# Old keys' probabilities of all four row tiles turned by way of memory, the new keys first in every chunk

## The chip, the core and the metric

One core of one Trainium2 chip. The metric is the device time of one execution in microseconds (us), the median of several runs. TensorE multiplies matrices, VectorE (DVE), ScalarE (ACT) and GpSimd (POOL) work element by element, SyncE (SP) issues every DMA of this kernel, in program order. TensorE writes its results to PSUM banks of 128 x 512 floats; everything else lies in on-chip memory (SBUF) or in DRAM.

## The reference

Four sequences ("batches") of 512 rows of 512 features. Layer norm, attention over 512 context rows (the "old" keys and values) and the 512 rows' own keys and values (the "new" ones), a gated residual, a second layer norm, a feed-forward block with sign weights, and a second residual:

```python
q, k_new, v_new = x @ wq.T, x @ wk.T, x @ wv.T          # x: layer norm of the rows
k = concatenate([k_cache, k_new]); v = concatenate([v_cache, v_new])
attn = softmax(q @ k.T / sqrt(512))
x = x + tanh(g_xattn) * ((attn @ v) @ wo.T)
hidden = relu((layernorm(x) @ sign(up).T) * up_scale)
x = x + tanh(g_ffn) * ((hidden @ sign(down).T) * down_scale * output_scale)
```

## The kernel before

Precision comes from splitting: an operand is kept as a high part, made by ACT (`..., HI`), and a low part, made by DVE or POOL (`..., LO` = value minus high part), and each product is three matmuls (`PASSES`, high-high, high-low, low-high). So each thing that TensorE uses passes through ACT and then DVE.

The program is written out by hand for each engine, batch after batch (`batch(b)`, b = 0 to 3), with semaphores between the engines. In one batch TensorE computes, in this order:

- scores (seven products in the manner of Strassen), whose sums DVE puts into `probs`; ACT makes the exponentials tile by tile in the order 2, 3, 0, 1;
- `v_jobs`: new values 0 and 1, 16 transposes of 128x128 that turn the new keys' probabilities of the four row tiles, values 2 and 3, then 8 transposes for the old keys' probabilities of tiles 0 and 1 (`turn_probs`, `TURN_ORDER`, `turn_job` at L665);
- the attention (L855 on): four chunks e of 128 features, each 12 matmuls over new and 12 over old keys, in two banks `proj[:, e % 2]`, so that chunk 2 can only begin when chunk 0 has been copied out;
- the output projection, 16 pieces of 3 matmuls, the first four of which need chunk 0, the next four chunk 1, and so on (`out_piece`);
- the keys and queries of the next batch, which need that batch's normed rows, `xT`.

Of the old keys' probabilities, tiles 2 and 3 are turned without TensorE. DVE transposes squares of 32x32 (`square_probs`, L1386) into `probs_squares`; SP stores them into DRAM so that the squares change places (`place_squares`, L446: four stores a tile, L451), and loads them again (L457) into `squares_placed`; ACT and DVE split them into `probsT` (`placed_out` L1094, `placed_low` L1390). TensorE waits for that ahead of the first product over old keys.

The layer norm of the next batch uses rows that are loaded already turned. Their means and inverse deviations ("facts") are stored to DRAM by SP (L478), loaded again over all partitions once that store has landed (L483, `all_facts`), and applied by two operations of DVE (`norm_turned`, L1435 and L1438); then ACT splits the result into `xT` (L1181) and DVE makes its low part (`next_rows_low`, L1443). In batch 0 SP comes to the facts after placing the squares (L495, L496), in batches 1 and 2 before. In batch 0 DVE's `norm_turned` stands after its copy of chunk 1 and `next_rows_low` after chunk 2, in batches 1 and 2 after chunks 0 and 1. In batches 1 and 2 DVE also norms and turns four row tiles of an earlier batch (`turn_pair_squares`).

In the last batch the output projection runs into the first group of the feed-forward block (`up_group(0, 0)`). Its right operands are sums and splits that DVE makes between its copies of the chunks (`right_sum` L1499, `right_low` L1503), and its first product waits for chunk 3's copy.

## Time and profile before

| | |
|---|---|
| median of 3 runs | 582.67 us (582.62 to 582.96) |
| the profiled execution | 583.08 us |
| its span, first to last instruction | 581.1 us |
| TensorE busy | 575.6 us, 99% |
| DVE, ACT, POOL busy | 392.0, 280.6, 117.8 us |
| chain that ended last | 98% TensorE |
| mean granted TensorE clock | 0.999 |
| DRAM traffic over the span | 95 GB/s |

The profile shows one execution. A span of a matmul in it overlaps the next one's, so a cadence is read from where groups start. In a timeline row, "[1.38 <-DMA ...]" says that the engine had been idle for 1.38 us and what ended it.

### The profile page before, as it was taken

To read this page: it belongs to the slowest core of one execution; us is meant where nothing else is said; L and a number is where in the kernel's file an instruction comes from. 1 tells how busy PE (TensorE), PEld (TensorE's weight loads), DVE (VectorE), ACT (ScalarE), POOL (GpSimd) and SP (SyncE) were. 2 spreads that over 40 slices of the span, in tenths; PEclk is the share of its full clock that TensorE was granted. 3 is DMA by queue.
4 is the path that set the end of the run, shared out by engine and by line. 5 is a ranking of instruction groups with operands and counts; after the bars stand their busy time and mean duration, and the time that the engine had idled before them with its cause. 6 is when DMAs were issued, how large, how long until landed. Compare 5 with 4: busy or idle time off the path is not lost.

```text
span 581.1 us, 6945 instructions
## 1 busy us (share of the span) xinstructions
PE 575.6 (99%) x2642; PEld 478.5 (82%) x2642; DVE 392.0 (67%) x552; ACT 280.6 (48%) x406; POOL 117.8 (20%) x111
## 2 busy tenths in 40 slices
PE   9999999999999999999999999999999999999997
PEld 7888888888888888888888888888888888888885
DVE  5889554587675587673587676777569644766654
ACT  3783522473322463322475455656458345555531
POOL 5006403003003003003002015242422012332002
PEclk9999999999999999999999999999999999999999
DMA  8714432024115055115124613283821311230011
GB/s 288 241 70 138 81 108 73 18 70 130 38 46 99 16 202 145 38 50 97 33 76 109 216 49 133 74 180 109 177 78 37 144 32 42 95 123 37 0 73 72
DMA packets 76352, 55.78 MB, mean 96 GB/s; under 512 B 54944, under 2 KB 59040, under 8 KB 75936
## 3 DMA queue, kind: packets, MB, share of 16 engines
q1 hardware_dynamic: 76320, 55.34, 32.4%
q8 instruction: 21, 0.34, 0.3%
q14 instruction: 11, 0.09, 0.1%
HBM read 42.74 MB, written 12.60 MB: 95 GB/s over the span
## 4 chain that ended last, share of the span: by engine, by line
PE 98%; DVE 1%; ACT 0%; issue 0%
PE proj L673 36%; PE score L791 19%; PE turn L776 12%; PE score L706 9%; PE score L673 7%; PE proj L776 5%; PE proj L706 4%; PE score L916 2%; PE turn L665 1%; PE score L665 1%; PE score L923 1%; DVE rows L1775 1%; DVE scaled L1772 0%; ACT four_x L1008 0%; PE proj L665 0%; ACT weights L1000 0%
## 5 line engine op out<-in xcount | busy, mean ns | idle before, releaser
L791 PE MATMUL score<-down_signs,hid_split 128*128 128x512 f32 x512 | 133.4, 389 | 0.0
L791 PEld LDWEIGHTS score<-down_signs,hid_split 128*128 128x128 f32 x512 | 96.0, 188 | 20.3 <-DVE hid_split L1656 0.5
L673 PE MATMUL proj<-probsT,four_x 128*128 128x512 f32 x384 | 88.1, 390 | 0.0
L673 PEld LDWEIGHTS proj<-probsT,four_x 128*128 128x128 f32 x384 | 71.8, 188 | 14.7
L673 PE MATMUL proj<-four_x,weights 128*128 128x512 f32 x336 | 76.8, 389 | 0.0
L673 PEld LDWEIGHTS proj<-four_x,weights 128*128 128x128 f32 x336 | 63.0, 188 | 13.0
L597 POOL TENSOR_TENSOR four_x<-raw_ctx,four_x 128x2048 fp32r<-128x2048 f32 x7 | 32.6, 4656 | 147.9 <-ACT four_x L1004 147.9
L1656 DVE TENSOR_TENSOR hid_split<-hid,hid_split 128x512 fp32r<-128x512 f32 x64 | 44.3, 695 | 15.5 <-ACT hid_split L1218 15.4
L776 PE MATMUL turn<-ops_b,up_ops 128*128 128x512 f32 x192 | 51.3, 389 | 0.0
L1012 ACT ACTIVATE four_x<-proj 128x512 fp32r<-128x512 f32 x32 | 19.0, 593 | 65.4 <-PE proj L673 65.4
L1218 ACT ACTIVATE hid_split<-hid 128x512 fp32r<-128x512 f32 x64 | 40.0, 630 | 20.9 <-PE score L791 18.1
L1209 ACT ACTIVATE hid<-hid,hid_gain 128x512 f32<-128x512 f32 x48 | 34.8, 724 | 22.7 <-DVE hid L1685 11.1
L673 PE MATMUL proj<-weights,four_x 128*128 128x512 f32 x192 | 45.4, 392 | 0.0
L673 PE MATMUL score<-weights,four_x 128*128 128x512 f32 x192 | 45.3, 389 | 0.0
L1301 DVE TENSOR_TENSOR four_x<-proj,four_x 128x512 fp32r<-128x512 f32 x32 | 21.9, 686 | 31.5 <-ACT four_x L1012 31.5
L776 PEld LDWEIGHTS turn<-ops_b,up_ops 128*128 128x128 f32 x192 | 36.0, 188 | 7.5
L673 PEld LDWEIGHTS score<-weights,four_x 128*128 128x128 f32 x192 | 36.0, 188 | 7.5
L634 POOL TENSOR_TENSOR up_ops<-up_ops 128x256 fp32r<-128x256 f32 x16 | 14.3, 891 | 136.8 <-ACT up_ops L1112 136.8
L673 PEld LDWEIGHTS proj<-weights,four_x 128*128 128x128 f32 x192 | 35.8, 188 | 7.3
L1085 ACT ACTIVATE probs<-probs,neg_max 128x1024 f32<-128x1024 f32 x16 | 18.4, 1153 | 34.4 <-DVE neg_max L1376 34.4
L1368 DVE TENSOR_TENSOR probs<-score,probs 128x512 f32<-128x512 f32 x40 | 27.5, 686 | 10.8 <-PE score L706 10.1
L776 PE MATMUL proj<-ops_a,up_ops 128*128 128x512 f32 x128 | 34.2, 389 | 0.0
(136 smaller groups left out, 861.1 us busy)
## 6 DMA issues: line engine op xcount, KB each, us to landing
raw_w<-in_ffn_w SPq DMA_DIRECT2D x21, 512.0 KB, 3.3
raw_ctx<-in_ctx_turned SPq DMA_DIRECT2D x4, 1024.0 KB, 5.3
raw_ctx<-in_ctx SPq DMA_DIRECT2D x4, 1024.0 KB, 5.3
raw_x<-block_rows SPq DMA_DIRECT2D x4, 1024.0 KB, 6.0
result<-rows SPq DMA_DIRECT2D x16, 256.0 KB, 2.0
rows<-in_x SPq DMA_DIRECT2D x3, 1024.0 KB, 8.2
turned_x<-in_x_turned SPq DMA_DIRECT2D x3, 1024.0 KB, 5.3
probs_rows<-probs_squares SPq DMA_DIRECT2D x32, 64.0 KB, 2.3
```

The source lines that it names most:

```text
L597: pool.tensor_tensor(ctx_side[:, LO], raw_ctx[:, :, :], ctx_side[:, HI].bitcast(F32), ALU.subtract).then_inc(ctx_ready, 1)
L673: last = pe.matmul(bank, lhs(l), rhs(r), start=start and i == 0, stop=stop and i == 2)
L706: last = pe.matmul(score_bank(i, t), q_left(i, l)[:, c, t * P:(t + 1) * P], key_right(SCORE_RIGHT[i], r)[:, c, :], start=i in (A11, S3, S2 ...
L776: last = pe.matmul(bank, up_ops[:, g % 2, left, c * P:(c + 1) * P], right(i)[:, s, c, :], start=start and c == 0 and s == HI, stop=stop an ...
L791: last = pe.matmul(wide(r), hid_split[:, n % HR, s, r * P:(r + 1) * P], down_signs[:, chunk_of(q), :], start=(q == 0 and s == HI), stop=(q ...
L1012: act.activation(dst, proj_bank(n), ACT.Copy).then_inc(proj_hi, 1)
L1085: act.activation(probs[:, t, :], probs[:, t, :], ACT.Exp, bias=neg_max[:, t:t + 1], accum_out=row_sum[:, t:t + 1]).then_inc(exp_done, 1)
L1209: act.activation(dst, src, ACT.Relu, scale=hid_gain[:, j:j + 1]).then_inc(relu_done, 1)
L1218: act.activation(hid_split[:, n % HR, HI, :], src, ACT.Copy).then_inc(hid_hi, 1)
L1301: dve.tensor_tensor(dst(LO), proj_bank(proj0(b) + i), dst(HI).bitcast(F32), ALU.subtract).then_inc(proj_lo, 1)
L1368: dve.tensor_tensor(dst, bank, plus, ALU.add).then_inc(score_sums, 1)
L1656: dve.tensor_tensor(hid_split[:, n % HR, LO, :], src, hid_split[:, n % HR, HI, :].bitcast(F32), ALU.subtract).then_inc(hid_ready, 1)
```

## The change

The old keys' probabilities of all four tiles take the way through memory, in two parts (`PAIRS`: tiles 2 and 3, then 0 and 1). The eight transposes of old keys go, with their copies on ACT and DVE. DVE makes squares of four tiles, SP stores 16 times and then loads each part with one DMA of 512 KB. `probs_squares` grows to all four tiles, over the high parts of old keys, so the copy of the first part waits until every store of squares has landed.

In the attention, all four chunks take their 12 matmuls over new keys first, then each its 12 over old keys; chunks 2 and 3 use the two turn banks. TensorE waits for both parts ahead of the first product over old keys.

On DVE the low part of the first placed part comes after value 3's copy, that of the second after the row gains and the block statistics. `norm_turned` moves ahead of all four chunk copies in each of batches 0 to 2, `next_rows_low` behind chunk 0's, `turn_pair_squares` behind chunk 1's. ACT splits `xT` after chunk 0. In the last batch ACT takes one block of signs before chunk 0's copy. SP's order of calls is as before.

```diff
@@ -42,7 +42,7 @@
     W_O, W_K, W_Q, W_V = range(4)
-    TURNS_BATCH = 2 * RT - 2
+    TURNS_BATCH = RT
     TURNS_ALL = RT + TURNS_BATCH * BATCH
@@ -154,18 +154,23 @@
         SQ = 32
-        SQUARED = (2, 3)
         pair_normed = at("pair_normed", 192, [P, RT, DIM])
         pair_squares = at("pair_squares", 200, [P, RT, DIM])
         late_normed = at("late_normed", 200, [P, 2, DIM])
         late_squares = normed
-        probs_squares = at("probs_squares", 164, [P, len(SQUARED), ROWS])
+        PAIRS = ((2, 3), (0, 1))
+        probs_squares = at("probs_squares", 160, [P, RT, ROWS])
         squares_placed = at("squares_placed", 176, [P, KC, ROWS])
-        probs_rows = nc.dram_tensor("probs_rows", (BATCH, len(SQUARED), ROWS, P), F32).ap()
-        probs_rows_v = probs_rows.rearrange("b t (c p) q -> b t p c q", p=P)
-        probs_squares_v = probs_rows.rearrange("b t (j n) (i a) -> b t i n j a", n=SQ, a=SQ)
+        probs_rows = nc.dram_tensor("probs_rows", (BATCH, ROWS, ROWS), F32).ap()
+        probs_rows_v = probs_rows.rearrange("b (c p) q -> b p c q", p=P)
+        probs_squares_v = probs_rows.rearrange("b (j n) (t i a) -> b t i n j a", n=SQ, i=P // SQ, a=SQ)
+
+        def placed_part(h):
+
+            first = PAIRS[h][0] * P
+            return slice(None), slice(0, RT), slice(first, first + 2 * P)
         def scaled(c, r):
@@ -227,7 +232,11 @@
             return turn[:, n % 4, :] if n % 4 < 2 else score[1][:, n % 4 - 2, :]
         def proj_bank(n):
-            return wide(n) if n < DC else proj[:, n % 2, :]
+            if n < DC:
+                return wide(n)
+
+            i = (n - PROJS_FIRST) % PROJS_BATCH
+            return turn[:, i - 6, :] if n >= PROJS_FIRST and i in (6, 7) else proj[:, n % 2, :]
         small_in, ctx_in, out_stored = map(sem, ("small_in", "ctx_in", "out_stored"))
         x0_in = [sem(f"x0_in{i}") for i in range(RT)]
...
...
@@ -356,7 +362,6 @@
         TILE_ORDER = (2, 3, 0, 1)
         OLD, NEW = 0, 1
-        TURN_ORDER = ((2, NEW), (3, NEW), (0, NEW), (1, NEW), (0, OLD), (1, OLD))
         T_SUMS, T_HI, T_LO = (T1, T3, T2, T4), (T1, T3, T2, T4, B22), (T3, T1, T2, T4, B22)
         S_SUMS, S_HI, S_LO = (S3, S2, S4, S1), (A11, S3, A12, S2, S4, S1), (A11, S3, A12, S2, S1, A22, S4)
@@ -445,16 +450,18 @@
             def place_squares(b):
-                for k, t in enumerate(SQUARED):
-                    sp.wait_ge(probs_squared, len(SQUARED) * b + k + 1)
-                    for i in range(P // SQ):
-                        sp.dma_start(probs_squares_v[b, k, i], probs_squares[i * SQ:(i + 1) * SQ, k].rearrange(
-                            "n (j a) -> n j a", a=SQ)).then_inc(probs_out_done, 16)
+                for h, pair in enumerate(PAIRS):
+                    for t in pair:
+                        sp.wait_ge(probs_squared, tile_done(b, t))
+                        for i in range(P // SQ):
+                            sp.dma_start(probs_squares_v[b, t, i], probs_squares[i * SQ:(i + 1) * SQ, t].rearrange(
+                                "n (j a) -> n j a", a=SQ)).then_inc(squares_stored[h], 16)
                 sp.wait_ge(scored, product_scored(b, A22, 1))
-                for k, t in enumerate(SQUARED):
-                    sp.wait_ge(probs_out_done, STORED * len(SQUARED) * (b + 1))
-                    sp.dma_start(squares_placed[:, 0:RT, t * P:(t + 1) * P], probs_rows_v[b, k]).then_inc(placed, 16)
+                for h, pair in enumerate(PAIRS):
+                    sp.wait_ge(squares_stored[h], 2 * STORED * (b + 1))
+                    cols = slice(pair[0] * P, (pair[1] + 1) * P)
+                    sp.dma_start(squares_placed[placed_part(h)], probs_rows_v[b][:, :, cols]).then_inc(placed[h], 16)
             def block_rows_back(b):
                 sp.wait_ge(squares_out[b], STORED)
@@ -687,10 +694,11 @@
             def v_terms(r):
                 return [(out_of(xT, c, r * P, (r + 1) * P), out_of(weights[:, W_V], c, 0, DIM)) for c in range(DC)]
-            def attn_terms(e):
-                new = [(out_of(new_side, r, e * P, (e + 1) * P), out_of(probsT, DC + r, 0, ROWS)) for r in range(RT)]
-                old = [(out_of(ctx_side, r, e * P, (e + 1) * P), out_of(probsT, r, 0, ROWS)) for r in range(RT)]
-                return new, old
+            def new_terms(e):
+                return [(out_of(new_side, r, e * P, (e + 1) * P), out_of(probsT, DC + r, 0, ROWS)) for r in range(RT)]
+
+            def old_terms(e):
+                return [(out_of(ctx_side, r, e * P, (e + 1) * P), out_of(probsT, r, 0, ROWS)) for r in range(RT)]
             def score_bank(i, t):
@@ -744,9 +752,9 @@
                     score_product(b, S4, t)
             def turn_probs(b, i):
-                t, side = TURN_ORDER[i]
+                t = TILE_ORDER[i]
                 pe.wait_ge(exp_done, tile_done(b, t))
-                turn_job(turn0(b) + i, cols(probs[:, t, side * 512:(side + 1) * 512]))
+                turn_job(turn0(b) + i, cols(probs[:, t, ROWS:KEYS]))
             def v_jobs(b):
@@ -763,9 +771,6 @@
                     if r == 1:
                         pe.wait_ge(score_sums, 10 * (b + 1))
                         for i in range(RT):
-                            turn_probs(b, i)
-                    if r == 3:
-                        for i in range(RT, TURNS_BATCH):
                             turn_probs(b, i)
             def up_product(g, k, bank, left, i, start, stop):
@@ -851,25 +856,21 @@
                 n = proj0(b)
                 pe.wait_ge(turn_lo, turn0(b) + RT)
-                for e, side in ((0, NEW), (1, NEW), (0, OLD), (1, OLD), (2, NEW), (2, OLD), (3, NEW), (3, OLD)):
-                    new, old = attn_terms(e)
-                    if side == NEW:
-                        if e >= 1:
-                            pe.wait_ge(proj_lo, values_out(b, DC + e - 2))
-                        for i, (lhs, rhs) in enumerate(new):
-                            if e == 0:
-
-                                pe.wait_ge(proj_lo, values_out(b, max(i, 2)))
-                            last = product(proj[:, e % 2, :], lhs, rhs, i == 0, False)
-                        if last_batch and e == DC - 1:
-                            last.then_inc(new_read, 1)
-                        continue
-                    if e == 0:
-                        pe.wait_ge(turn_lo, turn0(b) + TURNS_BATCH)
-                        pe.wait_ge(placed_lo, b + 1)
-                        pe.wait_ge(ctx_ready, values_split(b) + 1)
-                    for i, (lhs, rhs) in enumerate(old):
-                        last = product(proj[:, e % 2, :], lhs, rhs, False, i == RT - 1)
+                for e in range(DC):
+                    if e == 1:
+                        pe.wait_ge(proj_lo, values_out(b, 3))
+                    for i, (lhs, rhs) in enumerate(new_terms(e)):
+                        if e == 0:
+
+                            pe.wait_ge(proj_lo, values_out(b, max(i, 2)))
+                        last = product(proj_bank(n + DC + e), lhs, rhs, i == 0, False)
+                if last_batch:
+                    last.then_inc(new_read, 1)
+                pe.wait_ge(placed_lo, 2 * b + 2)
+                pe.wait_ge(ctx_ready, values_split(b) + 1)
+                for e in range(DC):
+                    for i, (lhs, rhs) in enumerate(old_terms(e)):
+                        last = product(proj_bank(n + DC + e), lhs, rhs, False, i == RT - 1)
                     last.then_inc(proj_done, 1)
                 def out_piece(i):
@@ -1086,12 +1087,16 @@
                                bias=neg_max[:, t:t + 1], accum_out=row_sum[:, t:t + 1]).then_inc(exp_done, 1)
             def probs_out(b, i):
-                t, side = TURN_ORDER[i]
-                turn_out(turn0(b) + i, probsT[:, HI, 4 * side:4 * side + 4, t * P:(t + 1) * P])
-
-            def placed_out(b):
-                act.wait_ge(placed, 16 * len(SQUARED) * (b + 1))
-                act.activation(probsT[:, HI][PLACED], squares_placed[PLACED], ACT.Copy).then_inc(placed_hi, 1)
+                t = TILE_ORDER[i]
+                turn_out(turn0(b) + i, probsT[:, HI, RT:KC, t * P:(t + 1) * P])
+
+            def placed_out(b, h):
+                act.wait_ge(placed[h], 16 * (b + 1))
+                part = placed_part(h)
+                if h == 0:
+
+                    act.wait_ge(squares_stored[1], 2 * STORED * (b + 1))
+                act.activation(probsT[:, HI][part], squares_placed[part], ACT.Copy).then_inc(placed_hi, 1)
             def take_signs(n):
                 kind, i = SIGNS[n]
@@ -1147,14 +1152,11 @@
                     probs_out(b, i)
                 proj_out(m + 2, new_side[:, HI, 2, :])
                 proj_out(m + 3, new_side[:, HI, 3, :])
-
-                act.wait_ge(probs_out_done, STORED * len(SQUARED) * (b + 1))
-                for i in range(RT, TURNS_BATCH):
-                    probs_out(b, i)
-                placed_out(b)
+                placed_out(b, 0)
+                placed_out(b, 1)
                 if last_batch:
+                    take_signs(3)
                     proj_out(m + 4, qT[:, HI, 0, :])
-                    take_signs(3)
                     right_high(0, B11)
                     proj_out(m + 5, qT[:, HI, 1, :])
                     right_high(0, B21)
@@ -1176,7 +1178,7 @@
                         weight_high(W_O, i)
                 for e in range(DC):
                     proj_out(m + 4 + e, qT[:, HI, e, :])
-                    if e == (2 if b == 0 else 1):
+                    if e == 0:
                         act.wait_ge(turned_normed, b + 1)
                         act.activation(xT[:, HI], turned_x[:, :, :], ACT.Copy).then_inc(next_hi, 1)
                 context_high(turned_split(b + 1))
@@ -1376,18 +1378,19 @@
                 dve.reduce_max(neg_max[:, t:t + 1], probs[:, t, :], AX.X, negate=True).then_inc(max_done, 1)
             def probs_out(b, i):
-                t, side = TURN_ORDER[i]
-                turn_out(turn0(b) + i, lambda s: probsT[:, s, 4 * side:4 * side + 4, t * P:(t + 1) * P])
-
-            def square_probs(b, k):
-                dve.wait_ge(exp_done, tile_done(b, SQUARED[k]))
-                if k == 0:
-                    dve.wait_ge(scored, product_scored(b, S2, 1))
-                dve.transpose(probs_squares[:, k, :], probs[:, SQUARED[k], 0:ROWS]).then_inc(probs_squared, 1)
-
-            def placed_low(b):
-                dve.wait_ge(placed_hi, b + 1)
-                dve.tensor_tensor(probsT[:, LO][PLACED], squares_placed[PLACED], probsT[:, HI][PLACED].bitcast(F32),
+                t = TILE_ORDER[i]
+                turn_out(turn0(b) + i, lambda s: probsT[:, s, RT:KC, t * P:(t + 1) * P])
+
+            def square_probs(b, t):
+                dve.wait_ge(exp_done, tile_done(b, t))
+                if t == TILE_ORDER[0]:
+                    dve.wait_ge(scored, product_scored(b, S1, 1))
+                dve.transpose(probs_squares[:, t, :], probs[:, t, 0:ROWS]).then_inc(probs_squared, 1)
+
+            def placed_low(b, h):
+                dve.wait_ge(placed_hi, 2 * b + h + 1)
+                part = placed_part(h)
+                dve.tensor_tensor(probsT[:, LO][part], squares_placed[part], probsT[:, HI][part].bitcast(F32),
                                   ALU.subtract).then_inc(placed_lo, 1)
             def keys(b):
@@ -1529,24 +1532,24 @@
                 sum_scores(b, AT_C21, 1)
                 sum_scores(b, AT_C12, 0)
                 maxima(b, 3)
-                square_probs(b, 0)
+                square_probs(b, 2)
                 maxima(b, 0)
-                square_probs(b, 1)
+                square_probs(b, 3)
                 sum_scores(b, AT_C12, 1)
                 maxima(b, 1)
+                square_probs(b, 0)
                 proj_out(b, 0, chunk(new_side, 0))
                 if b == 0:
                     norm_stats(RT + 3, 1)
                     norm_moments(1)
                     means(1)
+                square_probs(b, 1)
                 proj_out(b, 1, chunk(new_side, 1))
                 for i in range(RT):
                     probs_out(b, i)
                 proj_out(b, 2, chunk(new_side, 2))
                 proj_out(b, 3, chunk(new_side, 3))
-                for i in range(RT, TURNS_BATCH):
-                    probs_out(b, i)
-                placed_low(b)
+                placed_low(b, 0)
                 dve.wait_ge(exp_done, RT * b + RT)
                 dve.reciprocal(row_inv[:, :], row_sum[:, :]).then_inc(inv_done, 1)
                 dve.wait_ge(inv_done, b + 1)
@@ -1560,6 +1563,8 @@
                 if last_batch:
                     block_row_stats(2 * RT)
                     block_row_moments(2)
+                placed_low(b, 1)
+                if last_batch:
                     proj_out(b, 4, chunk(qT, 0))
                     right_low(0, B11)
                     proj_out(b, 5, chunk(qT, 1))
@@ -1576,14 +1581,12 @@
                     right_low(0, T2)
                     right_low(0, T4)
                 else:
+                    norm_turned(b + 1)
                     for e in range(DC):
                         proj_out(b, DC + e, chunk(qT, e))
-
-                        if e == (1 if b == 0 else 0):
-                            norm_turned(b + 1)
-                        if e == (2 if b == 0 else 1):
+                        if e == 0:
                             next_rows_low(b + 1)
-                        if e == 2 and b >= 1:
+                        if e == 1 and b >= 1:
                             turn_pair_squares(b - 1)
                 if last_batch:
```

## Rows read from the trace of the kernel before

**Rows 1.** The page's table of engines: busy us (share of span) xinstructions.

```profile
PE 575.6 (99%) x2642; PEld 478.5 (82%) x2642; DVE 392.0 (67%) x552; ACT 280.6 (48%) x406; POOL 117.8 (20%) x111
```

**Rows 2.** Timeline, TensorE, batch 0: start us, us, engine, line, op, out<-in, count.

```profile
58.93 5.73 PE L673 MATMUL proj<-weights,four_x 128*128 128x512 f32 x24
64.50 1.03 PE L665 MATMUL turn<-ident,probs 128*128 128x128 f32 x8
65.29 22.02 PE L673 MATMUL proj<-probsT,four_x 128*128 128x512 f32 x96
87.15 11.04 PE L673 MATMUL score<-weights,four_x 128*128 128x512 f32 x48
98.03 21.92 PE L673 MATMUL proj<-four_x,weights 128*128 128x512 f32 x96
```

**Rows 3.** Timeline of SP's queue in batch 0; the length is the issuing.

```profile
54.03 6.48 SPq L451 DMA_DIRECT2D probs_rows<-probs_squares  x8
62.07 0.93 SPq L457 DMA_DIRECT2D squares_placed<-probs_rows  x2
63.09 0.45 SPq L478 DMA_DIRECT2D row_facts<-mean_rstd  x1
73.18 0.34 SPq L483 DMA_DIRECT2D all_facts<-row_facts  x1
73.57 0.43 SPq L498 DMA_DIRECT2D rows<-in_x  x1
```

**Rows 4.** DMA issues between 60 and 84 us: count, KB each, us to landing.

```profile
squares_placed<-probs_rows SPq DMA_DIRECT2D x2, 256.0 KB, 3.0
all_facts<-row_facts SPq DMA_DIRECT2D x1, 512.0 KB, 6.0
...
row_facts<-mean_rstd SPq DMA_DIRECT2D x1, 4.0 KB, 10.1
```

**Rows 5.** Timeline of batch 0, DVE, ACT and POOL.

```profile
65.33 0.69 DVE L1301 TENSOR_TENSOR four_x<-proj,four_x 128x512 fp32r<-128x512 f32 x1 [2.03 <-ACT four_x L1012]
...
66.17 1.06 ACT L1094 ACTIVATE probsT<-squares_placed 128x1024 fp32r<-128x1024 f32 x1
...
67.26 1.23 DVE L1390 TENSOR_TENSOR probsT<-squares_placed,probsT 128x1024 fp32r<-128x1024 f32 x1
67.92 5.46 POOL L592 TENSOR_TENSOR weights<-rows,weights 128x512 fp32r<-128x512 f32 x4 [8.15 <-ACT weights L1000]
...
79.17 2.29 DVE L1435 TENSOR_TENSOR turned_x<-turned_x,all_facts 128x2048 f32<-128x2048 f32 x1 [1.38 <-DMA all_facts<-row_facts]
81.49 2.29 DVE L1438 TENSOR_TENSOR turned_x<-turned_x,all_facts 128x2048 f32<-128x2048 f32 x1
...
83.82 1.92 ACT L1181 ACTIVATE four_x<-turned_x 128x2048 fp32r<-128x2048 f32 x1 [1.31 <-DVE turned_x L1438]
...
85.77 2.29 DVE L1443 TENSOR_TENSOR four_x<-turned_x,four_x 128x2048 fp32r<-128x2048 f32 x1 [1.38 <-ACT four_x L1181]
```

**Rows 6.** Timeline of batch 1, the squares' stores and the attention's start.

```profile
140.20 4.09 SPq L451 DMA_DIRECT2D probs_rows<-probs_squares  x8
...
151.51 1.03 PE L665 MATMUL score<-ident,probs 128*128 128x128 f32 x8
...
152.31 7.97 PE L673 MATMUL proj<-probsT,four_x 128*128 128x512 f32 x34
```

**Rows 7.** DMA issues between 84 and 130 us, batch 1's among them.

```profile
all_facts<-row_facts SPq DMA_DIRECT2D x1, 512.0 KB, 3.6
row_facts<-mean_rstd SPq DMA_DIRECT2D x1, 4.0 KB, 15.1
```

**Rows 8.** Timeline of the last batch, DVE and TensorE.

```profile
347.78 1.75 DVE L1499 TENSOR_TENSOR raw_x<-raw_x 128x1024 f32<-128x1024 f32 x1
...
349.46 0.68 DVE L1301 TENSOR_TENSOR four_x<-proj,four_x 128x512 fp32r<-128x512 f32 x1
...
353.63 1.07 PE L776 MATMUL proj<-ops_a,up_ops 128*128 128x512 f32 x4
```

5 lines of the change are left out of this document (2 added, 3 removed).

## The prediction

> **What bounds the kernel now.** I read the page's engine table first. TensorE is busy for 575.6 of 581.1 us [rows 1], and after the start its timeline carries no mark of idle time. So an edit pays only by what it takes from TensorE's own stream, and costs whatever it makes TensorE wait. Next the timeline of TensorE in batch 0 [rows 2]: from 58.93 to 98.03 each group starts where the one before it ends. The reader should take the cadence from there: 48 matmuls of L673 start at 87.15 and the next group at 98.03, so one matmul costs 10.88 / 48 = 0.2267 us (the 11.04 us shown are a modelled, overlapping length). Then the timeline of the queue of DMAs (SP), its landings, and VectorE (DVE) and ScalarE (ACT) in the same batch [rows 3, 4, 5], because the change puts new work there. The granted clock is full throughout (mean 0.999), so it is no term.
>
> **What is removed: eight transposes a batch.** Values 2 and 3 (24 matmuls, 5.44 us) start at 58.93, and the removed transposes at 64.50, 5.57 later. The attention begins at 65.29. Its 96 matmuls need 21.76 us and take 21.86. The transposes thus occupy 0.79 us and their group change another 0.10 us: 0.89 a batch [rows 2]. Batch 1 shows the same 0.80 between its marks, 151.51 and 152.31 [rows 6], as do batches 2 and 3. Four times 0.89 is **3.56 us**. ACT and DVE also lose two copies each a batch, which is worth nothing while TensorE sets the end.
>
> **The new order on TensorE.** The same 96 matmuls run, 48 over new keys, then 48 over old. In batch 0 they start at 64.50, the old keys at 64.50 + 10.88 = 75.38, and the output products at 86.26. The first product's fourth term needs value 3, whose low part DVE finishes at 66.02 [rows 5], against 64.50 + 9 x 0.2267 = 66.54. It fits by half a microsecond. The extra banks are free: TensorE waits before the attention, as it did, until both turn banks are emptied.
>
> **Do the squares come in time?** SP now issues 16 stores of 64 KB instead of 8 before it places anything. In batch 0 the first 8 end at 54.03 + 6.48 = 60.51; in batch 1 eight take 4.09, about 0.5 each [rows 3, 6]. The longer time in batch 0 is a queue behind the load of the next rows, issued just before. Squares of tiles 0 and 1 leave DVE before SP is free, so the second 8 take 4.2 (bounds 4.0 and 6.5) and end at 64.7. The first placing load goes at once; the second waits for the last landing. Before, placing began 1.56 us after the last store [rows 3], so now at 66.3. It lands some 3.6 later (a 512 KB load, all_facts, landed in 3.6 in batch 1 [rows 7]; two of 256 KB in 3.0 [rows 4]) at 69.9. ACT's copy of 128x1024 takes 1.06 and DVE's low part 1.23 [rows 5], with ACT's tanh and DVE's row gain between them: about 73. TensorE asks at 75.38. Covered by some 2 us. In batches 1 to 3 the first store leaves 12 us before the attention starts (140.20 against 152.31 [rows 6]), and even behind DVE's block statistics, which now stand ahead of the second low part, about 3 us are left. Cost nothing; without that cover each microsecond of lateness is one of TensorE's.
>
> The Trainium skill advises against this route. "VectorE: DVE Perf Modes", section "Rules for kernel authors", sends a full 128x128 transpose to TensorE, and its section "The three transpose paths" calls a strided plain DMA 19 times slower. Here 64 KB in 128-byte runs leave every 0.5 us, about 130 GB/s [rows 6], which is no such factor; if stores were several times slower, every batch would wait and the sum would be far above the kernel before.
>
> **What is queued behind: the row facts of batch 1.** This is the term I think decides. In batch 0 alone, SP issues the store of the row facts (mean and 1/std) after the placing, and the load that spreads them over all partitions after that store has landed. Before: 63.09, landed 10.1 later, all_facts issued 73.18, landed 6.0 later at 79.17, where DVE's norm_turned had waited 1.38 us [rows 3, 4, 5]. Now the store goes after the second placing load: 66.3 + 0.5 = 66.8, a delay of 3.7. Landing again 10.1 gives 76.9. Bounds for all_facts are 3.6 (alone, batch 1) and 6.0 (with the 1 MB load of batch 2's rows issued 0.4 us behind it). That load now comes about 0.6 behind, since POOL's output weights (5.46 us from 67.92 [rows 5]) move with ACT to about 77.5. I take 5.5, near its own row. The facts are there at **L = 82.4** (bounds 80.5 and 85).
>
> The change also moves norm_turned ahead of DVE's four copies of the attention's chunks, in batch 0 too, where it was behind two. So those queue behind the facts. From L: two operations, 4.61 to their end (79.17 to 81.49 + 2.29), chunk 0's low part 0.7; meanwhile ACT splits xT (1.92) and then DVE makes its low part (2.29) and chunk 1's low part (0.7), together 4.9 after norm_turned [rows 5]. Chunk 0 is wanted at 86.26 and needs L + 5.5; chunk 1 is wanted 2.72 later, 88.98, and needs L + 9.5 + 0.2 for TensorE to load. The sum of both waits is L - 79.3 = **3.1 us**. Before, with the same L, nothing waited, as chunks 0 and 1 were copied first. Chunks 2 and 3 follow in time. In batches 1 and 2 SP handles the facts ahead of the squares, so they are there long before; norm_turned fits into the 48 matmuls of old keys, and the four normed and turned tiles of the pair, now before chunk 2's copy, end about 2.5 us ahead of need. Nothing there.
>
> **The last batch.** Chunk 0 is ready 4.5 us later than before (after 60 matmuls, not 36, less the 0.89), and behind it DVE has a packed list: chunk copies, four sums and lows of B11, B21, B22, T1, all before chunk 3's low part, for which the first up product waits. That product stood at 353.63, chunk 3's copy ended at 350.15 [rows 8]. Chunk 1 now ends 48 matmuls, 10.88 us, before the wanted 353.63 - 0.89 = 352.74, at 341.9; ACT has copied it at 342.7. From there DVE has no gap: chunk copies 1, 2 and 3 at 0.7, and seven low parts and sums at 1.2 (a low part of that size is in [rows 5]; one sum took 1.75 with POOL at work beside it [rows 8]), and a wait of about 0.4 for ACT. That is 10.9 us, 353.6, plus 0.2 for TensorE to load: 1.06 late; 10.2 if the operations overlap a little more, 11.6 with POOL in the way. I take **1.0 us** (bounds 0.3 and 1.8).
>
> **Sum.** -3.56 + 3.1 + 1.0 = +0.5. The profiled execution took 583.08 (span 581.1 and 1.98 around it), 0.41 above the median of 582.67; the difference is applied to the median: 583.2. A measurement here can tell about 0.2%, 1.2 us, from no change.
>
> **Rivals.**
> (a) The facts aren't late. If all_facts lands in 3.6 as in batch 1 [rows 7], L = 80.5 and the wait is 1.2. With 0.5 in the last batch: -3.56 + 1.7 = -1.9, 580.8; with no wait at all 579.1. For it: the only other one shown took 3.6. Against it: the one of batch 0 took 6.0, with the same follower.
> The Trainium skill, "DMA: Bandwidth & Descriptors", section on the anatomy of one DMA, gives a fixed 2.0 us plus bytes over bandwidth, by which the 4 KB store of the facts would land in 2 us and no wait would be left (an estimate: 579.1 to 580.1). The rows say 10.1 and 15.1 [rows 4, 7], so this adds only a few hundredths to (a). Chance of (a) 0.25.
> (b) Slower: the store of the facts lands later than 10.1 us after its issue. It took 15.1 where a 1 MB load was ahead of it [rows 7]; now two 512 KB loads are, before two of 256 KB. Every microsecond is paid in full; it decides from L = 83.1 on. Midway, at 12 us for the store, L = 84.3, wait 5.0: +2.4, 585.1. Chance 0.25.
> (c) Slower: the placed squares, not the facts, come last. If the second 8 stores also take 6.5 us in batch 0, placing and facts both move 2.3 more: 585.5. Chance 0.05.
> (d) The near balance as summed, 583.2, own range 581.6 to 584.4. Chance 0.45.
>
> **Numbers.** The range takes in (d), the nearer half of (a), and (b) to its middle: 580.6 to 585.8. Faster by over 0.2%: 0.25. Within: 0.45. Slower: 0.30.
>
> **What the profile after would show.** Values 2 and 3 followed at once by 96 matmuls, in each batch. Batches 1 and 2 each shorter by 0.89; else the cover of the squares failed. The first idle time of TensorE after 16 us, in batch 0 at the output products, about 1.8 and 1.3 us, released by DVE's four_x copies behind norm_turned, and L near 82.4. A wait of about 1 us at the first up product. The forecast is wrong if row_facts lands much sooner or later than 10 us, or if L1435 doesn't start when all_facts lands.

## The result, and the profile after

The changed kernel takes 587.85 us, the median of 6 executions (584.59 to 589.02), against 582.62 (582.51 to 582.96) of the kernel before on the same chip. The ratio is 1.0079 [1.005, 1.0109]: slower by 0.8%. The forecast was 583.2, and the measured time is 2 us above the top of the predicted range. The profiled execution is one of the shorter ones, 585.54 us with a span of 583.7; before it was 583.08 with 581.1.

First the page of the kernel after: the table of engines (busy us, share of the span, instructions) and the granted clock in 40 slices.

```profile
span 583.7 us, 6905 instructions
...
PE 574.2 (98%) x2610; PEld 476.2 (82%) x2610; DVE 395.7 (68%) x556; ACT 281.0 (48%) x402; POOL 124.9 (21%) x111
...
PEclk9999989999999999999999999999999999999999
```

Against [rows 1] TensorE has 32 instructions fewer, the transposes, and is busy 1.4 us less, yet the span is 2.6 us longer. One slice of 40, the sixth (73 to 88 us, batch 0), shows a lower clock. Before, none did. TensorE's waits over the whole kernel after (engine, product, line, releaser: total us, times, longest) are two, besides 1.2 us at the end and 0.2 at the start that every version has:

```profile
PE proj L680 <- DVE probsT L1393: 2.4, 1, 2.4
PE proj L781 <- issue: 1.7, 1, 1.7
```

The first is a wait for the placed squares, the second the first up product of the last batch. TensorE's timeline, batch 0 first and then a mark of each later batch (start us, us, engine, line, tile, shapes, count, idle before and releaser):

```profile
58.89 5.73 PE L680 MATMUL proj<-weights,four_x 128*128 128x512 f32 x24
64.45 5.60 PE L680 MATMUL proj<-probsT,four_x 128*128 128x512 f32 x24
69.89 5.60 PE L680 MATMUL turn<-probsT,four_x 128*128 128x512 f32 x24
77.91 7.34 PE L680 MATMUL proj<-probsT,four_x 128*128 128x512 f32 x24 [2.42 <-DVE probsT L1393]
85.09 5.60 PE L680 MATMUL turn<-probsT,four_x 128*128 128x512 f32 x24
90.53 11.04 PE L680 MATMUL score<-weights,four_x 128*128 128x512 f32 x48
101.41 21.92 PE L680 MATMUL proj<-four_x,weights 128*128 128x512 f32 x96
123.17 2.88 PE L714 MATMUL proj<-four_x 128*128 128x512 f32 x12
...
209.26 2.88 PE L714 MATMUL proj<-four_x 128*128 128x512 f32 x12
...
295.38 2.88 PE L714 MATMUL proj<-four_x 128*128 128x512 f32 x12
...
348.83 5.60 PE L680 MATMUL score<-weights,four_x 128*128 128x512 f32 x24
356.14 1.16 PE L781 MATMUL proj<-ops_a,up_ops 128*128 128x512 f32 x4 [1.71 <-issue]
```

New keys run from 64.45 to 75.33 (48 x 0.2267), as forecast. Then TensorE stands until 77.91. The 24 matmuls behind the wait take 85.09 - 77.91 = 7.18 us instead of 5.44. Set beside [rows 2], from values 2 and 3 to the output products: 90.53 - 58.89 = 31.64 us against 28.22, that is +3.42 = -0.89 (transposes gone) + 2.58 (idle) + 1.74 (slow matmuls), with 0.01 left by rounding. Batches 1 and 2 take 86.09 and 86.12 between their marks, 0.92 and 0.90 less than before. In the last batch the product of [rows 8] comes 60.76 us after the mark instead of 59.81: due at 348.83 + 5.44 = 354.27, it starts at 356.14, 1.87 late less 0.89. In all +3.43 - 0.92 - 0.90 + 0.95 = +2.56, and the span grew by 2.6.

Why the squares are late is in the queue of DMAs (SP; the length is the issuing) and in the chain of what released what, both of batch 0, after:

```profile
53.99 12.34 SPq L457 DMA_DIRECT2D probs_rows<-probs_squares  x16
66.43 1.80 SPq L464 DMA_DIRECT2D squares_placed<-probs_rows  x2
68.33 0.45 SPq L485 DMA_DIRECT2D row_facts<-mean_rstd  x1
78.89 0.34 SPq L490 DMA_DIRECT2D all_facts<-row_facts  x1
...
67.85 7.38 DMA squares_placed<-probs_rows
75.22 0.02 issue
75.25 1.06 ACT probsT L1099
...
76.64 1.23 DVE probsT L1393
77.87 0.04 issue
77.91 7.34 PE proj L680 x24
```

The issuing of the stores ends at 66.33 instead of 60.51 [rows 3]. SP waits for the last of them to land, the second placing load leaves at 67.85, and it lands 7.38 us later, where those of [rows 4] took 3.0. Behind it stand ACT's copy, DVE's low part, and TensorE. The rest of the chain is short; one load carries the wait.

The clock by stretches of 3 us, after (us; busy of PE, PEld, DVE, ACT, POOL with instructions; granted clock; DMA share; GB/s):

```profile
72.00:75.00 3.00, 3.00 (x15) 2.50 (x14) 1.07 (x2) 0.00 (x0) 0.00 (x0) 1.00 0.05 0
75.00:78.00 3.00, 0.58 (x4) 0.16 (x2) 1.36 (x2) 2.75 (x6) 1.01 (x1) 1.00 0.00 0
78.00:81.00 3.00, 3.00 (x9) 2.37 (x10) 0.00 (x0) 0.48 (x1) 3.00 (x3) 0.64 0.05 14
81.00:84.00 3.00, 3.00 (x12) 2.38 (x12) 0.89 (x1) 0.60 (x1) 1.72 (x2) 0.79 0.52 173
```

The clock is full while TensorE idles, and falls just after it has resumed; the mean of a stretch lies between its two levels, 2.4 and 1.2 GHz. The row from 78 to 81 counts 9 matmuls, where a row at full speed counts 15. The last two numbers of a row are worth a look too: from 72 to 78 the DMA engines move next to nothing, though the second placing load is said to land only at 75.22.

The execution profiled is short of the median by 2.3 us. The six executions spread over 4.4 us with mean clocks of 0.998 down to 0.994, where the kernel before spreads over 0.45 us. Which wait grew in the other five can't be read without their traces; the experiments bear on it.

### The profile page after: what moved, and what is told of

It reads as the page before. It is cut to its first block, busy times and chain, and to the rows that moved or that the text cites. A ratio compares the mean times of both kernels' runs of the same rounds, so it can differ in the third digit from the quotient of the medians.

```text
span 583.7 us, 6905 instructions
## 1 busy us (share of the span) xinstructions
PE 574.2 (98%) x2610; PEld 476.2 (82%) x2610; DVE 395.7 (68%) x556; ACT 281.0 (48%) x402; POOL 124.9 (21%) x111
## 4 chain that ended last, share of the span: by engine, by line
PE 93%; DVE 2%; DMA 2%; SPq 1%; issue 1%; ACT 0%; DVEq 0%
PE proj L680 26%; PE score L796 19%; PE turn L781 12%; PE score L714 9%; PE score L680 7%; PE turn L680 7%; PE proj L781 5%; PE proj L714 4%; PE score L917 2%; DMA squares_placed<-probs_rows 1%; SPq L457 1%; PE score L924 1%; PE turn L672 1%; DMA probs_rows<-probs_squares 1%; DVE rows L1778 1%
## 5 line engine op out<-in xcount | busy, mean ns | idle before, releaser
L680 PE MATMUL proj<-probsT,four_x 128*128 128x512 f32 x192 | 46.6, 400 | 2.4 <-DVE probsT L1393 2.4
L680 PEld LDWEIGHTS proj<-probsT,four_x 128*128 128x128 f32 x192 | 37.1, 194 | 10.7 <-DVE probsT L1393 2.8
L680 PE MATMUL turn<-probsT,four_x 128*128 128x512 f32 x192 | 44.8, 389 | 0.0
L680 PEld LDWEIGHTS turn<-probsT,four_x 128*128 128x128 f32 x192 | 36.0, 188 | 7.5
L1013 ACT ACTIVATE four_x<-proj 128x512 fp32r<-128x512 f32 x24 | 14.2, 590 | 42.9 <-PE proj L680 42.9
```

The source lines that it names most:

```text
L680: last = pe.matmul(bank, lhs(l), rhs(r), start=start and i == 0, stop=stop and i == 2)
L1013: act.activation(dst, proj_bank(n), ACT.Copy).then_inc(proj_hi, 1)
```

## The experiments

Two explanations were set against each other at first: **S**, the placed squares of batch 0 and the clock behind their wait cost the time; **F**, the row facts do, the term that the prediction thought decisive. Each ratio below is to the kernel before, run beside it on the same chip (medians 582.79 to 582.84).

**again** is the changed kernel unchanged.

> The changed kernel itself, for its spread and a second trace. Theory C (a wait of TensorE of about 2 us is followed by a stretch at the 1.2 GHz level, and how many waits have one differs from execution to execution): times between 584 and 589 again, and the granted clock falls only right behind the two waits, at batch 0's first product over old keys and at the first up product. Theory N (the clock has nothing to do with the waits): low stretches elsewhere, or none in a slow execution.

Measured: 586.55 us (4 executions), 1.007 [1.0055, 1.0085]. Its trace shows the wait for the squares at 3.88 us, with the later placing load landing 9.1 us after its issue. The same program thus waits 2.4 us in one execution and 3.9 in another. Its up product waits 1.71 as before, and only the stretch behind the first wait shows a low clock, not both as expected.

**norm_back** gives DVE its old order in batch 0, and ACT its split of `xT` behind chunk 2 as before, so that late facts hold back fewer copies. The cut shows DVE's part.

```
-                    norm_turned(b + 1)
+                    if b > 0:
+                        norm_turned(b + 1)
                     for e in range(DC):
                         proj_out(b, DC + e, chunk(qT, e))
-                        if e == 0:
+                        if b == 0 and e == 1:
+                            norm_turned(b + 1)
+                        if e == (2 if b == 0 else 0):
                             next_rows_low(b + 1)
```

> The changed kernel, but in batch 0 norm_turned stands behind chunk 1's copy and next_rows_low behind chunk 2's, as before the change. Theory F (the facts of batch 1 decide batch 0, as predicted): batch 0 some 3 us shorter, median about 584. Theory S (the second part of the placed squares comes last and TensorE waits for it, 2.4 us in the trace): the wait is the same, the time the same as the changed kernel's within its spread.

Measured: 586.44 (10 executions, 583.11 to 587.57), 1.0053 [1.0035, 1.0071]. In its trace TensorE's waits are those of **again**, 3.9 us for the squares and 1.7 at the up product. F falls. The two shortest executions, 583.11 and 583.36, have a mean clock of 0.999, which fits a shorter wait for the squares with no low clock behind it. They weren't traced, and that the wait was gone isn't shown: rows_late, without it, takes 581.53.

**rows_late** is norm_back with SP's order in batch 0 changed: the 1 MB load of the turned rows of batch 1 (`next_rows(1)`) behind the stores, the placing and the facts.

```
-                    next_rows(1)
                     place_squares(0)
                     next_facts(1)
+                    next_rows(1)
```

> norm_back, and in batch 0 SP loads the turned rows of batch 1 behind the facts and not ahead of the squares' stores. Theory S: 16 stores in about 9 us instead of 12.3, the second part placed 3 us earlier, no wait of TensorE in batch 0 and no low clock there: batch 0 ends 3.4 + 0.9 us earlier than now, median near 582 to 583 with what is left in the last batch. Theory F, the facts or now the rows behind them late: TensorE waits at the output products instead, 584 or more.

Measured: 581.53 (10 executions), 0.9978 [0.9969, 0.9987]. The stores now take 8.56 us, 0.53 each, as in batch 1 [rows 6], and the placing is issued 5 us sooner. Of the 5 us, 1.2 is an earlier start. In the kernel after, the issue of the fifth store takes 2.28 us and that of the last 1.72; here none takes over 0.52.

```profile
52.78 8.56 SPq L457 DMA_DIRECT2D probs_rows<-probs_squares  x16
61.44 1.69 SPq L464 DMA_DIRECT2D squares_placed<-probs_rows  x2
```

The load still lands 8.0 us after its issue, but in time: no wait in batch 0, clock full. The 4.9 us less than norm_back from the place of one load are S, with its clock term.

**stall_a** measures the clock by itself: the kernel before, with idle reductions on DVE ahead of the squares' low part in batches 1 and 2, sized for two different waits.

```
+                if DELAY[b]:
+                    dve.wait_ge(idle_set, 1)
+                    dve.reduce_max(idle_out[:, b:b + 1], idle_in[:, 0:1].broadcast_to([P, DELAY[b]]), AX.X)
                 placed_low(b)
```

with `DELAY = (0, 3200, 4400, 0)`.

> The kernel before with one idle reduction on DVE ahead of the placed squares' low part in batch 1 (3200 elements, about 3.3 us) and batch 2 (4400, about 4.6 us), whose results nothing uses. TensorE should wait about 1.1 us in batch 1 and 2.3 us in batch 2. Theory N: +3.4 us, 586.1, clock full. Theory C: a stretch at the low level behind the longer wait, 1.7 us more or so, 587.8, and the clock row shows whether 1.1 us alone brings it about.

Measured: 587.45 (4 executions), 1.0075 [1.006, 1.009]. TensorE's timeline at the two waits, and the clock around the second:

```profile
158.15 16.60 PE L676 MATMUL proj<-probsT,four_x 128*128 128x512 f32 x72 [0.85 <-issue]
...
247.55 18.11 PE L676 MATMUL proj<-probsT,four_x 128*128 128x512 f32 x72 [2.10 <-issue]
...
244.00:247.00 3.00, 1.45 (x7) 0.87 (x5) 3.00 (x2) 0.00 (x0) 0.00 (x0) 1.00 0.00 0
247.00:250.00 3.00, 2.45 (x6) 2.00 (x7) 2.96 (x7) 0.00 (x0) 0.00 (x0) 0.57 0.00 0
```

72 matmuls need 16.32. Behind 0.85 us of idle time the next group starts 16.44 later, and next to nothing is lost. Behind 2.10 it starts 17.94 later, 1.62 lost. The sum 0.85 + 2.10 + 1.62 = 4.57 is near what the span grew by (4.3) and the median (4.6). The clock term thus needs no late DMA; a wait of TensorE on DVE has the same price.

**facts_after** asks why the load lands so late. It is norm_back with SP waiting for the placed squares before it issues the 4 KB store of the facts.

```
                     place_squares(0)
+                    sp.wait_ge(placed[1], 16)
                     next_facts(1)
```

> norm_back, and in batch 0 SP waits until the second part of the squares has landed before it stores the row facts. Theory Q (the 4 KB store of the facts, in 4-byte pieces right behind the second placing load, holds that load's landing back: 7.4 to 9.1 us in batch 0 of four traces, 3.8 to 4.7 in the other batches, where nothing of the kind follows): it lands in 4 to 4.7 us, and TensorE's wait for the squares goes; the facts come 4 us later, so chunk 3's copy behind next_rows_low may make it wait up to 1.5 us at the output products. Theory L (the landing is late because of what went ahead, 16 stores and the 1 MB load): 7 us or more again, the wait of 2.4 to 3.9 us as it was.

Measured: 584.51 (5 executions), 1.0029 [1.0017, 1.0041]. Landings of all eight placing loads, and TensorE's waits:

```profile
DMA to landing us min/median/max: 4.1/4.4/5.1
...
PE score L681 <- DVE four_x L1304: 2.3, 2, 1.3
PE proj L782 <- issue: 1.7, 1, 1.7
```

Against 7.4 of the kernel after, no load now takes over 5.1, and the squares' wait is gone. The facts come 5 us later instead and cost 2.3 us at the output products, in two waits so short that the clock stays full (1.0 in the profiled execution; one of the other four has 0.996). The loads and all that went ahead of them are the same, so it took the store behind them to make the landing late.

**rows_late_only** moves the rows' load alone, with DVE's order as in the change, to test the prediction's facts term.

> The changed kernel with only SP's order in batch 0 altered (the turned rows of batch 1 behind the facts), norm_turned still ahead of all chunk copies. The squares are in time; now the step of the prediction can be seen by itself. If it was sound, norm_turned starts when facts and rows are there, about 81, and TensorE waits in all 1.3 to 1.9 us at the output products, in two pieces: 1.5 us slower than rows_late, near 583. If it was not, the time is rows_late's, 581.5.

Measured: 585.07 (4 executions), 1.0037 [1.0022, 1.0051], 2 us more than expected: the placing load took 11.3 us this time, and TensorE waited 1.68 for the squares. The arithmetic behind norm_turned could still be read. It began at 83.21, held back here by the turned rows, which this edit loads late, and not by the facts, which had landed at 80.5. The old keys ended at 88.26, and the output products waited in two places.

```profile
88.53 2.97 PE L680 MATMUL score<-weights,four_x 128*128 128x512 f32 x12 [0.27 <-issue]
92.75 8.46 PE L680 MATMUL score<-weights,four_x 128*128 128x512 f32 x36 [1.26 <-DVE four_x L1303]
```

By the prediction's steps the second chunk is ready at 83.21 + 9.7 = 92.91 and wanted at 88.26 + 2.72 = 90.98, 1.9 us in all; it started at 92.75, 1.8 late.

**last_old** is the change in batches 0 to 2 alone. **both** is that with the edits of rows_late.

```
+    OLD_WAY = (3,)
+    def turns(b):
+        return 2 * RT - 2 if b in OLD_WAY else RT
```

> The changed kernel in batches 0 to 2; the last batch works as before the change (transposes of tiles 0 and 1, chunks 0 and 1 finished first). The wait at the first up product, 1.7 us in the traces, should go, and with it its 0.89 us of gain: 0.9 us shorter in a trace of one clock dip, and executions with a granted clock of 0.994 no longer seen, so a median of 584.5 to 585.5 against the changed kernel's 586.6 to 587.9.

> rows_late and last_old together: no wait of TensorE after the start, three batches shorter by 0.89. 582.7 - 2.7 = 580.0, with the small spread of the kernel before. If the stores and loads of the squares cost TensorE anything outside its waits, it is more than that.

Measured: last_old 587.02 (4 executions), 1.0068 [1.0054, 1.0082]; both 581.08 (12 executions), 0.9971 [0.996, 0.9982]. Both are above what was expected, 584.5 to 585.5 and 580.0. In last_old the up product no longer waits, but the profiled execution had a longer wait in batch 0, with its load landing after 10.6 us:

```profile
80.97 7.80 PE L697 MATMUL proj<-probsT,four_x 128*128 128x512 f32 x24 [5.55 <-DVE probsT L1441]
...
78.00:81.00 3.00, 0.03 (x1) 0.04 (x1) 1.36 (x2) 2.70 (x6) 0.95 (x1) 0.59 0.00 0
```

The expectation that a mean clock of 0.994 belongs to the last batch's wait missed: it is here without that wait. With 5.55 us idle the clock is down before TensorE resumes, and 2.19 us are lost behind it (88.60 - 80.97 - 5.44). Executions of the kernel after with 0.994, at 588.7 to 589.0, fit such a wait; that is argued, not traced. In both's profiled execution, its longest, the load took 11.7 us and the squares waited 2.05, even with the rows' load moved.

**best** holds the facts' store back and keeps the last batch as before; the rows' load goes out between that store and the wait for it. **best_last_new** is the same with the change in the last batch too.

```
                     place_squares(0)
+                    sp.wait_ge(placed[1], 16)
                     next_facts(1)
...
                              allow_slow_non_contiguous=True).then_inc(facts_stored, 16)
+                if b == 1:
+                    next_rows(1)
                 sp.wait_ge(facts_stored, 16 * b)
```

> both, and in batch 0 SP waits for the landing of the second part before it stores the row facts; the turned rows of batch 1 are loaded right behind that store. Theory Q says that nothing is then left that can be late: no wait of TensorE after the start in any execution, 582.8 - 2.7 = 580.1, with lowest and highest within 1 us, where both went from 579.8 to 583.5. If the spread stays, Q isn't its cause.

> The same SP and DVE order in batch 0, and the last batch in the new way. Against the run best it gives the price of the last batch alone: -0.89 for the transposes and +1.7 to +1.9 for the wait at the first up product, so 0.9 us slower, 581.0. If the new way paid in the last batch, it would be 0.9 faster.

Measured: best 581.87 (11 executions), 0.9982 [0.9973, 0.9991]; best_last_new 583.10 (11 executions), 1.0005 [0.9996, 1.0014]. The medians differ by 1.23 us. In the two traces the last batch, from its mark to the end of the span, takes 288.27 us with the change and 287.25 without, so 1.0 us is its price; the rest is in batch 0, whose order is the same in both. Best missed its 580.1, and its spread is 2.3 us where under 1 was expected: the facts' store, now with the 1 MB load behind it, landed after 12.6 us, norm_turned began at 85.45, and a chunk was late:

```profile
95.01 3.01 PE L699 MATMUL score<-weights,four_x 128*128 128x512 f32 x12 [0.85 <-DVE four_x L1353]
```

**four_loads** is norm_back with the two 512 KB placing loads cut into four of 256 KB, the size of [rows 4].

```
-                    sp.dma_start(squares_placed[placed_part(h)], probs_rows_v[b][:, :, cols]).then_inc(placed[h], 16)
+                    for t in pair:
+                        cols = slice(t * P, (t + 1) * P)
+                        sp.dma_start(squares_placed[:, 0:RT, cols], probs_rows_v[b][:, :, cols]).then_inc(placed[h], 16)
```

> norm_back, but each part of the squares is loaded by two DMAs of 256 KB, one for each row tile, as before the change; the store of the facts is again right behind the last. In the kernel before such a load landed in 3.0 us with that store behind it. If the late landing belongs to the 512 KB load: 3 to 4 us here, no wait for squares or one below 1 us, 583 to 584. If it belongs to what lies ahead in the queue or to the facts' store alone: 7 to 11 us again, 586 to 587.

Measured: 587.39 (10 executions, 582.5 to 589.7), 1.007 [1.0043, 1.0097]. The profiled execution is one of the longest, 589.62. Its first three loads in batch 0 landed after 3.3 to 4.2 us, the last after 10.7, and TensorE waited 6.13: the size of one load isn't the cause.

**before_16** is the kernel before with its eight stores repeated into memory that nobody reads: sixteen stores, two loads of 256 KB, the facts behind.

```
+                for k, t in enumerate(SQUARED):
+                    for i in range(P // SQ):
+                        sp.dma_start(spare_v[b, k, i], probs_squares[i * SQ:(i + 1) * SQ, k].rearrange(
+                            "n (j a) -> n j a", a=SQ)).then_inc(probs_out_done, 16)
```

> The kernel before, with the 8 stores of squares of each batch repeated into a DRAM tensor that nothing reads, so that 16 stores go ahead of the two placing loads, which wait for all of them; in batch 0 the facts' store follows right behind, as always. Read from the trace: the landing of the second placing load in batch 0. If the late landing in the changed kernel needs the longer row of stores ahead and the facts' store behind, it is 7 us or more here, and 3 to 4 in the other batches. If the number of stores has no part in it, it is 3 us as in the kernel before. TensorE will wait for the squares either way.

Measured: 589.84 (one execution). The second placing load of batch 0 landed after 5.1 us, between the 3 and the 7 of the two expectations. So sixteen stores ahead, with the facts' store behind, don't by themselves bring 7 to 12. TensorE still waited, as its old order wants the squares sooner:

```profile
75.38 18.57 PE L679 MATMUL proj<-probsT,four_x 128*128 128x512 f32 x72 [4.76 <-issue]
```

**best2** is best with the next rows' work on DVE and ACT behind one chunk more (`e == 2` for norm_turned, `3 if b == 0` for the next rows).

> best, with norm_turned of batch 0 behind chunk 2's copy and next_rows_low behind chunk 3's. best still waited 0.85 us for chunk 3's low part, which stood behind next_rows_low. Here no wait is left in batch 0: 0.9 to 1.3 us less than best, 580.5 to 581, and the spread of best (580.4 to 582.8), which I put down to this wait varying with the facts' landing, down to below 1 us.

Measured: 579.96 (11 executions, ten of them up to 580.96 and one of 583.72), 0.9959 [0.9947, 0.997], and a span of 577.8 in the profiled one. norm_turned waits 0.38 us, until 84.96, and TensorE waits nowhere between the start and the end. That is 0.4% or 2.85 us faster than the kernel before, all of the 3 x 0.89 = 2.67 that three batches' transposes are worth.

**mid_only** makes the change in batches 1 and 2 alone.

> The new way in batches 1 and 2 alone; batches 0 and 3 as before the change. Two times 0.89 less and nothing else: 582.8 - 1.8 = 581.0, with the spread of the kernel before (0.5 us). More than that would mean that the new way costs something in batches 1 and 2 too.

Measured: 581.05 (12 executions), 0.9975 [0.9967, 0.9984]: 1.76 us less, twice 0.88. The spread, 580.74 to 583.55, is wider than the 0.5 us expected; why isn't known. The trace shows no wait; in batch 0 its load, followed by the facts' store, landed in 4.9.

## Why the prediction was wrong

**Bound and what is removed: right.** Only TensorE's stream counts, and 0.89 us a batch went where no wait came in: 0.92 and 0.90 in batches 1 and 2, 1.76 for two in mid_only.

**"Do the squares come in time?": this step failed.** It gave them 2 us of cover; they were 2.5 late. Two terms were wrong. The first is when the stores have landed. All but the last left at the pace taken: the second eight start at 60.78 and then every 0.54 us, up to 64.61. But the issue of the last took 1.72 us, and the last two landed after 3.5 and 3.2 us, where stores just before them took 1.9 to 2.3. Two stretches of the stores (issue ns min/median/max, first and last start; under each the us to landing):

```profile
L457 SPq DMA_DIRECT2D probs_rows<-probs_squares x4: 488/512/513, 61.9 to 63.5; - x4
DMA to landing us min/median/max: 1.9/2.1/2.3
...
L457 SPq DMA_DIRECT2D probs_rows<-probs_squares x3: 488/511/1716, 63.5 to 64.6; - x3
DMA to landing us min/median/max: 2.3/3.2/3.5
```

In all the second eight took 5.55 us to issue, inside the bounds of 4.0 and 6.5, where 4.2 was taken, and the load left at 67.85 and not at 66.3. In rows_late, without the rows' load ahead, every store lands within 1.9. How that load, landed at 59.3 itself, reaches the last stores isn't shown. In again all sixteen left in 10.76 us, the forecast 10.7, and the load still left 13.65 us after the first store, against 13.86 here. The second term is the placing load's landing, 7.38 us and not 3.6. That was priced by what such a load costs alone, and no bound was given for the case that the change makes, two of them with a 4 KB store right behind. Issue 1.5 late, landing 3.8 late, and DVE is done at 77.87 against 73. That the squares come last is rival (c), given 0.05; but it had them late by slow stores alone, went on through the facts, and didn't have the late landing. That its 585.5 is the profiled 585.54 is chance.

**No term for the clock.** The prediction said that each microsecond of lateness costs TensorE one. Here 2.58 of idle time brought 1.74 more at 1.2 GHz, stall_a shows 2.10 with 1.62, last_old 5.55 with 2.19. The trace before could not show it, as TensorE had no wait there after 16 us; its full clock was that of an engine that never waited, and the prediction took it as given for one that does.

**The facts: right in size, hidden.** The store landed in 10.6 (10.1 taken), norm_turned began at 83.11 (82.4 forecast), and rows_late_only confirms the arithmetic from norm_turned on. But the squares' wait moved the output products from 86.3 to 90.53, and the chunk copies were then in time. The two waits overlap, and the prediction priced the facts with the squares at nothing. That its 3.1 us stands near the 2.58 us of idle time is chance: the wait is another one. The facts' real part was another: their store is what held back the squares' landing (facts_after).

**The last batch: too small.** 1.87 late against 1.0 taken, outside the upper bound of 1.8 by little. Three of DVE's seven sums and low parts there ran with POOL beside them, and the seven took 9.9 us, not 8.4:

```profile
350.95 1.72 POOL L643 TENSOR_TENSOR up_ops<-up_ops 128x256 fp32r<-128x256 f32 x1
352.00 1.76 DVE L1506 TENSOR_TENSOR ops_a<-raw_x,ops_a 128x1024 fp32r<-128x1024 f32 x1
352.75 1.60 POOL L646 TENSOR_TENSOR up_ops<-up_ops 128x256 fp32r<-128x256 f32 x1
353.68 1.76 DVE L1502 TENSOR_TENSOR raw_x<-raw_x 128x1024 f32<-128x1024 f32 x1
355.36 0.68 DVE L1303 TENSOR_TENSOR four_x<-turn,four_x 128x512 fp32r<-128x512 f32 x1
```

[rows 8] had one such sum at 1.75, and I took 1.2 for all. Net of the transposes the last batch loses: 0.95 in the trace, 1.0 between the traces of best and best_last_new.

**Two rules that it weighed.** The factor of 19 that the prediction takes from the Trainium skill ("VectorE: DVE Perf Modes", "The three transpose paths") compares a strided plain DMA with a transposing DMA, which no run here has, so it isn't tested; what is shown is that 64 KB stores in 128-byte runs left every 0.53 us in rows_late. The fixed 2.0 us (the Trainium skill, "DMA: Bandwidth & Descriptors", anatomy of one DMA) is a fit to DMAs issued by GpSimd. It doesn't describe the facts' store, which SP issues: 10.6 us here, 12.6 in best.

By its terms: -3.56 + 3.1 + 1.0 was forecast, and the profiled execution gave -3.56 + 2.58 + 1.74 + 1.87 = +2.6 on the span. The remaining 2.3 us to the median are other executions, whose batch 0 wasn't traced.

## What to carry to other kernels

When a step is moved behind more transfers, price its landing in the queue that the change makes, with what goes out right behind it, and give it the bounds of that case, not of the load alone. Add up waits of one engine one after the other in time, since the first moves the need of the second. Where TensorE has run without a break, a new wait can cost more than itself (2.58 us cost 4.3 here), so bound it with the clock term too. And a change that pays 0.9 us in each of four batches is worth making only in those that have the slack, which here were the middle two, and the first after its queue was put in another order.

## What the hardware showed that I had not expected

**A small store delays the landing of the load ahead of it.** The later placing load of batch 0 landed after 7.4, 9.1, 8.7, 8.0, 11.3, 10.6, 11.7 and 10.7 us in the eight traced executions with 1 MB of placing loads and the facts' store right behind them. With the store held back it took 5.1 (facts_after), 5.5 (best), 5.6 (best_last_new) and 5.6 (best2). With the store behind 0.5 MB of loads it took 3.2 (before and stall_a), 5.1 (before_16) and 4.9 (mid_only). In batches 1 to 3 of the kernel after, with nothing of the kind behind, it took 3.9 to 4.7. So in these runs the full delay needs both, the store behind and a megabyte queued. A load behind the store is late too: the 1 MB of turned rows landed after about 15 us in best, best_last_new and best2, where they go out right behind it, against 5.1 to 5.7 in the kernel after.

The packets in the traces show that the signal was late and not the data. In the kernel after, the load's last data packet ended at 71.98, and the landing was told 3.2 us later; in the other seven of the eight it was 3.6 to 6.7 us. This is all that the 16 DMA engines carried from 72.1 to 75.2, the remaining 4-byte packets of the facts' store:

```profile
DMA packets 153, 0.00 MB, mean 0 GB/s; under 512 B 153, under 2 KB 153, under 8 KB 153
```

With the store held back the landing was told 0.5 us after the last data packet, in all four. With 0.5 MB queued the lag was 0.5 us (before, stall_a), 1.7 (mid_only) and 2.3 (before_16), so a part of the delay is there too. What goes with the lag is how many of the store's some 1,070 packets had run before the load's last one ended: 415 to 578 in those four, 769 to 1,007 in the eight, none with the store held back.

The Trainium skill, "DMA: Bandwidth & Descriptors", section "Queues, rings and completion order", says that the semaphore increment is a strongly ordered write, which lands only after every earlier write from that DMA engine. The packet counts fit that, but no trace here shows when a single write is confirmed, so the reason stays open. Why it varies from one execution to the next (norm_back 583.1 to 587.6) is open too.

**Idle time and the clock.** Of TensorE's waits in these traces, those of 0.27 to 1.72 us left its clock at full speed; those of 2.05 (both), 2.10, 2.42, 3.88, 3.89, 4.76, 5.55 and 6.13 were each followed by a stretch at the lower level that cost 1.6 to 2.2 us. The price behind the wait hardly depends on its length.
